# Attention lags of a fused window-attention and convolution kernel: probabilities turned three units behind their scores, normalisation after the bias step, v one row later

## The reference, cut to what matters

```python
x = x + window_attention(group_norm(x))   # 7x7 windows, image rolled by 3 in both directions, 8 heads of 16 channels
x = x + conv3x3(group_norm(x), k)         # k: signs of w times a scale, times a mask
# window_attention, for each of the 64 windows (49 tokens) of an image:
qkv  = tokens @ qkv_weight.T + qkv_bias
attn = softmax(q * 16**-0.5 @ k.T + rel_pos_bias + mask)      # 8 heads, 49 x 49
out  = (attn @ v) @ proj_weight.T + proj_bias
```

## Time and profile before

| | |
|---|---|
| median of 3 executions | 3653.8 us (3641.2 to 3657.8) |
| the profiled execution, its own time | 3637.0 us |
| its span, first to last instruction | 3635.2 us |
| PE busy | 3190.5 us (88%) |
| DVE busy | 3073.1 us (85%) |
| ACT busy | 2555.1 us (70%) |
| POOL busy | 2365.1 us (65%) |
| mean granted clock of TensorE | 0.983 of full |

### The profile page before, as it was taken

One profiled execution on the slowest core, in us unless ns is written; L12 is line 12 of the kernel. 1 busy time (PEld: TensorE's weight loads), 2 busy tenths in 40 slices (PEclk: granted clock), 3 DMA queues, 4 the chain that ended last, 5 costly groups with the idle time before them and its releaser, 6 DMA issues.

```text
span 3635.2 us, 155064 instructions
## 1 busy us (share of the span) xinstructions
PE 3190.5 (88%) x64395; PEld 2684.8 (74%) x64395; DVE 3073.1 (85%) x6399; ACT 2555.1 (70%) x5729; POOL 2365.1 (65%) x3683
## 2 busy tenths in 40 slices
PE   2889989889899899898899999889898899898896
PEld 1667777777777777777777777777777777787775
DVE  5689888888888888888888888888888898888895
ACT  1667777767677777777777777777677777777772
POOL 4466666766667666667766667766667666667763
PEclk9999999999999999999999999999999999999998
DMA  2111111111111111111111111111111111111111
GB/s 57 37 42 52 47 42 47 49 50 49 37 47 50 49 52 47 42 47 50 52 52 50 42 45 49 50 52 50 37 47 50 50 52 47 42 47 50 34 35 36
DMA packets 260489, 169.26 MB, mean 47 GB/s; under 512 B 23120, under 2 KB 259792, under 8 KB 259792
## 3 DMA queue, kind: packets, MB, share of 16 engines
q1 hardware_dynamic: 259792, 159.34, 15.9%
HBM read 104.69 MB, written 54.59 MB: 44 GB/s over the span
## 4 chain that ended last, share of the span: by engine, by line
PE 33%; DVE 32%; issue 13%; POOL 9%; DMA 8%; ACT 4%; SPq 0%; DVEq 0%; ACTq 0%; POOLq 0%
PE conv_ps L1014 8%; DVE s_sb L766 6%; PE qkv_ps L895 6%; DMA recip_wide<-recip_dram 5%; PE attn_ps L932 4%; PE scores_ps L908 4%; PE attn_ps L936 4%; DVE plane_lo L778 3%; POOL s_sb L443 3%; DVE s_max L771 3%; DMA recip_dram<-recip 3%; DVE oT_lo L759 3%; PE probsT_ps L919 3%; DVE tok_lo L856 3%; DVE recip L746 2%
## 5 line engine op out<-in xcount | busy, mean ns | idle before, releaser
L443 POOL TENSOR_TENSOR s_sb<-s_sb,s_max 113x392 f32<-113x392 f32 x1024 | 998.9, 975 | 1092.7 <-DVE s_max L771 1091.4
L505 ACT COPY probsT<-probsT_ps 128x392 f32<-128x392 f32 x1024 | 490.8, 479 | 376.6 <-PE probsT_ps L919 366.4
L498 ACT ACTIVATE probs<-s_sb 113x392 f32<-113x392 f32 x1024 | 552.4, 539 | 221.1 <-POOL s_sb L443 218.6
L470 POOL TENSOR_TENSOR plane<-x_n 128x224 f32<-128x224 f32 x896 | 656.4, 753 | 18.7
L919 PE MATMUL probsT_ps<-ident,probs 113*128 113x113 f32 x4096 | 585.0, 265 | 38.7 <-ACT probsT L505 35.3
L771 DVE TENSOR_REDUCE s_max<-s_sb 113x8 f32<-113x392 f32 x1024 | 574.9, 561 | 35.3
L766 DVE TENSOR_TENSOR s_sb<-scores_ps,bias 113x392 f32<-113x392 f32 x1024 | 565.8, 552 | 41.0 <-PE scores_ps L908 37.1
L569 ACT COPY v<-qkv_ps 64x256 f32<-64x256 f32 (+2 forms) x1280 | 391.0, 325 | 211.6 <-PE qkv_ps L895 205.5
L1014 PE MATMUL conv_ps<-plane_hi,wc_hi 128*128 128x224 f16 x2688 | 484.4, 263 | 23.1 <-DVE conv_y L840 19.0
L919 PEld LDWEIGHTS probsT_ps<-ident,probs 113*128 113x128 f32 x4096 | 433.5, 141 | 90.7 <-ACT probs L498 47.9
L908 PE MATMUL scores_ps<-k,q 32*49 32x98 f32 x16384 | 477.4, 252 | 19.7 <-issue 19.4
(11 more groups left out here) (144 smaller groups left out, 6799.1 us busy)
## 6 DMA issues: line engine op xcount, KB each, us to landing
x_in<-in_x_dram SPq DMA_DIRECT2D x224, 224.0 KB, 3.9
recip_wide<-recip_dram SPq DMA_DIRECT2D x256, 196.0 KB
out_dram<-x_out SPq DMA_DIRECT2D x224, 224.0 KB, 2.3
recip_dram<-recip SPq DMA_DIRECT2D x256, 12.2 KB, 1.7
x<-in_L_conv_w_dram SPq DMA_DIRECT2D x1, 576.0 KB
x<-L_conv_pruning_mask_dram SPq DMA_DIRECT2D x1, 576.0 KB
x_n<-_conv_rel_pos_table_dram SPq DMA_DIRECT2D x14, 10.7 KB
x_n<-in_mask_dram SPq DMA_DIRECT2D x1, 196.0 KB
```

Of the source, the lines that this page charges most:

```text
L443: nc.gpsimd.tensor_tensor(s, s, top, ALU.subtract).then_inc(sub_ready, 1)
L470: last = nc.gpsimd.tensor_tensor(plane[:, t % 2, j], *sums[j])
L498: nc.scalar.activation(probs[0:QP, slot % 2, :, :, 0:N], s_sb[0:QP, slot % 4], ACT.Exp)\
L505: nc.scalar.copy(probsT[:, g % PT_SLOTS], probsT_ps[:].rearrange("p (w n) -> p w n", n=ODD)[:, :, 0:N])\
```

## The change

Five things are changed together.

1. `LAG_T` goes from 2 to 3: the probabilities of a unit are turned one step later, and `probs` gets a third buffer.
2. `values` runs at step 4r + 7, between the first two places of the convolution and `qkv`, and no longer at the end of step 4r + 5. The reciprocal runs in step 4r + 8, `o_sb` in 4r + 10, `oT_lo` in 4r + 11, the projection at the end of 4r + 11. On DVE these three now stand behind bias and maximum of their step; on ACT `oT_hi` stands behind the copy of `qkv_ps`.
3. v of row r is computed in the last two of row r's own four steps; q and k stay one row ahead. In the last of the four steps the run for window 7 of a row also covers window 0 of the next row, so there are four runs and not five, except in an image's last row. ACT's copies of v go to the slots of both rows.
4. The convolution begins at step 16 and not at 12, and its 36 matmuls are spread over the tile's four steps as 8, 18, 10, 0 and not as 6, 12, 6, 12.
5. The jobs of the second norm, the planes and the loads move by one to two steps.

The diff, cut to its core (lines that begin with @@ say where; `qkv_number` looks a job up in `QKV_ORDER`):

```diff
-LAG_T = 2
-VALUES_AT, NORMED_AT, SPLIT_AT = 5, 8, 9
+LAG_T = 3
+PROBS = 3
+VALUES_AT, RECIP_AT, NORMED_AT, SPLIT_AT = 7, 8, 10, 11
-PROJ_AT = 9
-G2_JOBS = ((6, END), (7, MID))
-NORM2_AT = 9
-VHI_AT, VLO_AT = 10, 12
-TIN_JOBS = ((10, END), (12, END), (14, MID), (14, END), (15, MID), (17, MID), (18, END))
+PROJ_AT = 11
+G2_JOBS = ((8, END), (9, MID))
+NORM2_AT = 10
+VHI_AT, VLO_AT = 11, 13
+TIN_JOBS = ((9, END), (10, END), (13, MID), (13, END), (14, END), (17, MID), (17, END))
-CONV_AT, CONV_STEPS = 12, 4
+CONV_AT, CONV_STEPS = 16, 4
-CONV_PARTS = ((0, 2, 4), (3, 4, 5), (2, 2, 2), (6, 6, 0))
+CONV_PARTS = ((0, 4, 4), (6, 6, 6), (4, 3, 3), (0, 0, 0))
...
+def qkv_job(i, u):
+    r, j = divmod(u, PAIRS)
+    if j < 2:
+        return live(i, 0 if r < ROWS - 1 else 1)
+    return live(i) or (i, u) == (-1, UNITS - 1)
+
+QKV_ORDER = {at: n for n, at in enumerate(at for at in product(range(-1, IMGS), range(UNITS)) if qkv_job(*at))}
+def k_number(row):
+    return qkv_number(*divmod((row - 1) * PAIRS + 1, UNITS))
+def v_number(row):
+    return qkv_number(*divmod(row * PAIRS + PAIRS - 1, UNITS))
...
-        probs = sb("probs", [128, 2, WP, 2, ODD])
+        probs = sb("probs", [128, PROBS, WP, 2, ODD])
@@ sync: body
-                    row = row_of(i, u, VALUES_AT + 1)
+                    row = row_of(i, u, RECIP_AT)
@@ scalar: exp_unit
-                need(act, probsT_ready, g - 1)
-                nc.scalar.activation(probs[0:QP, slot % 2, :, :, 0:N], s_sb[0:QP, slot % 4], ACT.Exp)\
+                need(act, probsT_ready, g - PROBS + 1)
+                nc.scalar.activation(probs[0:QP, g % PROBS, :, :, 0:N], s_sb[0:QP, slot % 4], ACT.Exp)\
@@ scalar: body; the block of oT_hi (NORMED_AT) moves from ahead of misc(MID) to behind misc(END)
-                    if live(i, 0 if r < ROWS - 1 else 1):
-                        number, slot = (i * ROWS + (r + 1)) * 4 + j, (r + 1) % 2
+                    if qkv_job(i, u):
+                        number, slot = qkv_number(i, u), (r + (j < 2)) % 2
...
-                            parts = ([(0, 4, 0, 0), (0, 4, 1, 1)] if j == 2 else
-                                     [(0, 4, 4, 0), (0, 3, 5, 1), (3, 1, 0, 1)])
+                            parts = [(0, 4, 0, 0, slot), (0, 4, 1, 1, slot)]
+                            if j == 3:
+                                parts = [(0, 4, 4, 0, slot), (0, 3, 5, 1, slot)] if live(i) else []
+                                if r < ROWS - 1 or live(i, 1):
+                                    parts.append((3, 1, 0, 1, 1 - slot))
@@ tensor: scores, turn_probs, values
-                    pe.wait_ge(qkv_free, (i * ROWS + r) * 4 + 2)
+                    pe.wait_ge(qkv_free, k_number(i * ROWS + r) + 1)
...
-                pe.wait_ge(qkv_free, (row + 1) * 4)
+                pe.wait_ge(qkv_free, v_number(row) + 1)
@@ tensor: qkv
-                row = (r + 1) % ROWS
+                row = (r + (j < 2)) % ROWS
...
-                    runs = [(b * C, slice(0, 128), (j - 2) * 4 + b) for b in range(4)]
-                    if j == 3:
-                        runs[3:] = [(3 * C, slice(0, ODD), NWIN - 1), (3 * C, slice(ODD, 128), 0)]
-                    for col, parts, w in runs:
-                        at, width = (row * NWIN + w) * ODD, parts.stop - parts.start
+                    runs = [(b * C, slice(0, 128), row * NWIN + (j - 2) * 4 + b) for b in range(4)]
+                    if j == 3 and r == ROWS - 1:
+                        runs[3:] = [(3 * C, slice(0, ODD), ROWS * NWIN - 1)] if live(i) else []
+                        if live(i, 1):
+                            runs.append((3 * C, slice(ODD, 128), 0))
+                        if not live(i):
+                            runs = runs[-1:]
+                    for col, parts, slot in runs:
+                        at, width = slot * ODD, parts.stop - parts.start
@@ tensor: body
                     conv(i, u, 1)
-                    if live(i, 0 if u // PAIRS < ROWS - 1 else 1):
+                    row = row_of(i, u, VALUES_AT)
+                    if row is not None:
+                        values(row)
+                    if qkv_job(i, u):
                         qkv(i, u)
                     conv(i, u, 2)
                     for job in misc_at(i, u, (END,)):
                         misc(i, u, *job)
-                    row = row_of(i, u, VALUES_AT)
-                    if row is not None:
-                        values(row)
```

More of the change, by code:

```diff
@@ L151, in row_of, with qkv_number @@
     return (i + turn) * ROWS + r if rest == 0 and live(i, turn) else None
+def qkv_job(i, u):
[4 more added lines that the diff above has]
+QKV_ORDER = {at: n for n, at in enumerate(at for at in product(range(-1, IMGS), range(UNITS)) if qkv_job(*at))}
+def qkv_number(i, u):
+    return QKV_ORDER[i, u]
+def k_number(row):
+    return qkv_number(*divmod((row - 1) * PAIRS + 1, UNITS))
+def v_number(row):
+    return qkv_number(*divmod(row * PAIRS + PAIRS - 1, UNITS))
 def roll_pieces(rows, row0=0):
@@ L562, in body @@
                         else:
-                            parts = ([(0, 4, 0, 0), (0, 4, 1, 1)] if j == 2 else
-                                     [(0, 4, 4, 0), (0, 3, 5, 1), (3, 1, 0, 1)])
+                            parts = [(0, 4, 0, 0, slot), (0, 4, 1, 1, slot)]
[3 more added lines that the diff above has]
+                                    parts.append((3, 1, 0, 1, 1 - slot))
                             vals = qkv_ps[:].rearrange("p (w a e d) -> p w a e d", w=NWIN // 2, e=2, d=HD)
-                            for b, n, w0, e in parts:
+                            for b, n, w0, e, to in parts:
                                 half = slice(ODD * e, ODD * e + ODD)
-                                last = nc.scalar.copy(v[half, slot, w0:w0 + n, :, e * HD:(e + 1) * HD],
+                                last = nc.scalar.copy(v[half, to, w0:w0 + n, :, e * HD:(e + 1) * HD],
                                                       vals[half, b:b + n, :, e, :])
@@ L572, in body @@
                     misc(i, u, END)
+                    row = row_of(i, u, NORMED_AT)
+                    if row is not None:
+                        act.wait_ge(o_ready, row + 1)
+                        need(act, oT_lo_ready, row)
+                        nc.scalar.copy(flat(oT_hi), flat(o_sb)).then_inc(oT_hi_ready, 1)
                     row = u - HI_AT
@@ L576, in body @@
                         act.wait_ge(gn1.applied, (i + 1) * ROWS + row + 1)
-                        need(act, qkv_ready, (i * ROWS + row + 1) * 4)
+                        if live(i):
+                            act.wait_ge(qkv_ready, v_number(i * ROWS + row) + 1)
                         nc.scalar.copy(
@@ L739, in body @@
                 for u in range(UNITS):
-                    row = row_of(i, u, VALUES_AT + 1)
+                    if live(i):
+                        g = i * UNITS + u
+                        dve.wait_ge(scores_ready, g + 1)
+                        need(dve, probs_ready, g - 3)
+                        edge = int(u // PAIRS == ROWS - 1)
+                        vec.tensor_tensor(s_sb[0:QP, u % 4].rearrange("p w h m -> p (w h m)"),
+                                          scores_ps[0:QP, u % 2, 0:WP * 2 * N],
+                                          bias[0:QP, edge, u % PAIRS].rearrange("p w h m -> p (w h m)"), ALU.add)\
+                            .then_inc(biased, 1)
+                        dve.wait_ge(biased, g + 1)
+                        vec.tensor_reduce(s_max[0:QP, u % 4], s_sb[0:QP, u % 4].rearrange("p w h m -> p (w h) m"),
+                                          AX.X, ALU.max).then_inc(max_ready, 1)
+                    row = row_of(i, u, RECIP_AT)
                     if row is not None:
```

21 lines of the change are left out of this document (2 added, 19 removed).

## The result

The changed kernel takes 4135.2 us (median of 4 executions, 4126.4 to 4139.6), the kernel before, on the same chip, 3650.5 (3641.2 to 3657.8). The ratio is 1.1326, with a 95% interval of 1.1291 to 1.1361. The direction was forecast, the size was not: 3910 was forecast, 485 us more came where 260 were expected, and the range to 4050 doesn't hold it.

A forecast was written before the change was run, and what follows sets the result against it. DVE and PE hold each other up. A row of 14.7 us (trip 5.5, other DVE work 8.4, x 0.5, gaps 0.3) against 13.68 adds 256, ends 3, to 3637, plus 17 for the median: 3910, range 3760 to 4050.

The forecast's parts named there:

- Waits removed: Per window row, PE's wait of values for probsT (0.50 us) and DVE's reciprocal wait for PE (0.62 us) would go.
- The trip as the main term, round trip 5.5 + rest 9.2: DVE, reciprocal to o_sb: 5.5 us DMA round trip covered by only 3.4 us of work, idle 2.1 us a row.
- I take the 5.5 of the earlier trace: Length of the reciprocal's DMA round trip, taken from one DVE timeline stretch; ends 5.1 and 7.3, mean at most 6.3.
- It runs its 26 matmuls beneath DVE's heavy step: no cost: PE's convolution while DVE does step 4r + 11 (oT_lo, projection, statistics, tile end): priced at nothing.
- some 2 us to spare: PE's slack before the scores of step 4r + 10, after about 7 us of work from the projection on.
- The rival built on PE being late: Bias of step 4r + 10 comes late after PE's 26 convolution matmuls, so waiting for scores covers the trip: 4%, 3950.
- x waits 0.5: DVE's addition to x waits 0.5 us a window row for the projection, where it was 0.20; bounds 0.25 and 0.85.
- Reaching break-even at a trip of 4.5: Rival "faster": a row is trip plus 9.2, equal to 13.68 at 4.5; without the x wait 13.2, 3530; 7%.
- PE's clock: Rival: PE, busy 83%, idles more and its clock falls; 10%.
- The range: 3760 to 4050, meant to hold most of the forecast, the clock rival and the late-PE rival; about 2 in 10 outside.
- high sum of 4280: Forecast's high end: trip 6.3, 0.85 at x and 0.4 for PE, 16.2 us a row; not expected to come together.
- Signs: If right: o_sb waits in nearly all 256 rows, 400 to 600 us; trip 5.5; DVE busy time within 2%; PE near 83%.

The follow-up runs named there:

- e2: Changed kernel with DVE's block that ends a convolution tile put ahead of projection and norms: 3908.8 us.
- e1: Changed kernel with o_sb multiplying by a constant tile and waiting for no DMA, so without normalisation: 3937.6 us.
- e17: Changed kernel with o_sb on a constant tile, waiting for no DMA, and convolution matmuls spread 8, 10, 18, 0: 3887.1 us.
- e6: Kernel before, its own lags kept, with DVE's reciprocal, o_sb and oT_lo put behind bias and maximum of their steps: 3943.6 us.
- e7: Changed kernel with the convolution begun at step 18 and the old spread 6, 12, 6, 12: 3871.3 us.
- e12: Changed kernel, long lags kept, with the old order on DVE and ACT (reciprocal, o_sb, oT_lo ahead of bias and maximum; oT_hi ahead of q's copy): 4060.1 us.
- e4: Changed kernel with the convolution's 26 matmuls of the first two steps all in the second (0, 26, 10, 0): 4153.3 us.
- e13: Changed kernel with the convolution's matmuls spread 8, 10, 18, 0 and not 8, 18, 10, 0: 4106.2 us.
- e18: Changed kernel with LAG_T 2, earlier values, reciprocal and o_sb, tile end ahead of projection; oT_lo put back behind bias and maximum: 3733.7 us, against 3735.9 with it ahead.

## Why the prediction was right and wrong, by its own steps

- *Waits removed*: right. No wait of `recip`, and `values` waits for `probsT` no more. But `values`, as the text had seen, now waits for `o_sb` of the row before (122.8 us), so PE gained little.
- *The trip as the main term, round trip 5.5 + rest 9.2*: the form held (6.13 + 9.48), and the cover of 3.4 us was right (DVE is busy for 3.39 us a row in that stretch). Both parts were short, by 0.63 and 0.28 us. Together that is 0.91 x 256 = 233 us, which is the miss (494 - 259 = 235).
- *"I take the 5.5 of the earlier trace rows"*: **the largest of the terms that were short.** Where the DMA set the stretch, in 148 of 216 rows, it took 5.86 us; 0.36 us a row, 92 us in all. The prediction had allowed up to 6.3 and took one row's value. Already in the kernel before, the 59 rows in which `o_sb` waited for the DMA had 5.93.
- *"It runs its 26 matmuls beneath DVE's heavy step: no cost"*: **the step whose reasoning failed.** PE's path was priced at nothing, from one window row for all eight. The other 0.27 us of the stretch (69 us in all) come from the 68 rows in which something else than the DMA was last, most of it from rows 0 and 1 of a turn, where bias and maximum of step 4r + 10 are done 7.42 and 6.36 us after the reciprocal. Two things hold PE there. The text looked only at what PE waits for at the scores; but the convolution's first matmul waits for `conv_ps` to be emptied, and the turned output for `result`, by the end of the tile, which stands last in DVE's heavy step (1.97 us in row 0, 1.56 in row 1; 0.8 to 1.2 in rows 3 to 7, where it costs nothing). Behind it come waits for ACT and for the norm, and a lower clock: 0.81 and 0.74 from 4 us before the reciprocal starts to `o_sb`, against 0.99 to 1.00 in rows 2 and 4 to 7. How much is due to each is open; e2 removes the wait for `conv_y`, and the waits for scores stay.
- In rows 2 and 4 to 7 the "some 2 us to spare" held: 1.3 to 2.1 us lie between that maximum and `o_sb`. There PE costs nothing while the trip is there; e1 and e17 show that it costs as soon as the trip goes. The rival built on PE being late was given 4%; it had rows 0 and 1 right and the rest wrong.
- *x waits 0.5*: 0.70, inside its bounds, and most of the 0.28 us by which the rest was short. e2 removes it and gains 226 us, of which its own length makes 179.
- *Reaching break-even at a trip of 4.5*: wrong. e1 has no trip and is at 14.93 us a row. "Rest" is no constant: as the stretch shrinks, it grows (9.48 to 10.27 in e17).
- *PE's clock* (10%): came true beside the rest, 0.93 against 0.98 to 0.99. PE is busy 0.87 us a window row longer. How much of this is on the chain is open: the clock doesn't order the times, since e6 has 0.965 at 3944 us and e7 0.946 at 3871. That idle is what lowers it was the author's assumption. The traces agree in direction: 0.99 where PE was busy 90% of the time (2524.26 of 2800 us), 0.93 where it was busy 85% (2705.81 of 3200 us, after). They don't show which is the cause, and a kernel that keeps PE busy artificially wasn't run. The 4050 of the range was set beside this rival. No run shows how much a lower clock adds to the sum; in its place the runs showed the 0.93, PE busy 13.20 us a window row against 12.33, and 1.56 us against 0.89 for the scores where the clock was 0.50.
- *The range*: its high sum of 4280 leaves out the 17 us that the forecast and the low end have; with them it is 4300. The range ended at 4050 because its long trip, full wait at x and late PE were taken not to come together. They came together in part: 5.86, 0.70 and 0.27.
- *Signs*: `o_sb` waited in 142 of 205 window rows, not nearly all, and 232 us, not 400 to 600; DVE's busy time rose by 0.8%, within the 2%; "DVE's wait moved to `s_sb` on `scores_ps`" was listed as what would make the forecast wrong. It did in part: both waits stand there, and in most rows the DMA comes last.

How much of the loss belongs to longer lags and how much to the moved convolution is open. Neither was run alone; e12 has both, and e7 moves the convolution within the changed kernel.

## What to carry to other kernels

Where a value leaves an in-order engine and comes back to it, draw the chain until it closes on itself, through every engine, and add it up: its length is a floor for the period whatever the lags are, and a block put one place back in one engine's list can lengthen it by all that it is put behind (three blocks put back cost 310 us here, 1.11 us a window row, where a bias and a maximum take 1.08). Do it for each kind of row: a mean over eight window rows hid that two of them were bound by another engine than the rest. For a moved step ask also which buffer it must find empty, and where in its engine's list the one who empties it stands. And a wait is no price: e4, e13 and e18 each lost or halved a large wait and kept their time within 1%. For e13, e17 shows that another floor lay beside it; for the other two that is argued from the waits that took its place.

## What the runs showed of the hardware

The slow form of `oT_lo` (mean 879 ns before, up to 1209) is gone after the change, and `plane_lo` has taken it over, from 642 ns to 915, from 500 to 3500 us (busy us, mean ns, idle):

```profile
L809 DVE TENSOR_TENSOR plane_lo<-plane,plane_hi 128x448 f16<-128x448 f32 x337 | 308.2, 915 | 0.0
L803 DVE TENSOR_TENSOR oT_lo<-o_sb,oT_hi 128x392 f16<-128x392 f32 x193 | 107.7, 558 | 0.0
```

In the two traces 639 of the 640 slow ones (over 640 ns, `tok_lo` among them) started with an operation of POOL already running. DVE's timeline has a `plane_lo` of each kind, and an `oT_lo`:

```profile
2219.63 0.62 DVE L809 TENSOR_TENSOR plane_lo<-plane,plane_hi 128x448 f16<-128x448 f32 x1
...
2229.95 0.56 DVE L803 TENSOR_TENSOR oT_lo<-o_sb,oT_hi 128x392 f16<-128x392 f32 x1
2230.42 1.27 DVE L809 TENSOR_TENSOR plane_lo<-plane,plane_hi 128x448 f16<-128x448 f32 x1
```

POOL's timeline:

```profile
2219.68 1.16 POOL L486 TENSOR_SCALAR x_n<-x,gn_y,gn_shift 128x448 f32<-128x448 f32 x1
...
2230.11 1.10 POOL L470 TENSOR_TENSOR s_sb<-s_sb,s_max 113x392 f32<-113x392 f32 x1 [0.75 <-DVE s_max L783]
```

The `plane_lo` at 2219.63 and the `oT_lo` start before POOL's operation and take 0.62 and 0.56 us beside it; the `plane_lo` at 2230.42 starts during it and takes 1.27, twice as long. From 500 to 3500 us of both kernels, 664 of the three remainders (`oT_lo`, `plane_lo`, `tok_lo`) start with POOL idle or within 50 ns of its operation's end, and all but one (675 ns) take 552 to 621 ns. 875 start while POOL has more to do; 639 of them take over 640 ns, up to 1445. The number of POOL's operands did not decide it: `tok_lo` took 818 ns or more in each of the 52 cases in which a one-operand operation (L482) was running. The slow form moved to whichever instruction now starts behind POOL's, and DVE's busy time (11.83 and 11.96 us a window row) doesn't show it.
